# Attention heads of a fused transformer layer: key-major probabilities from a second score matmul, instead of transposing query-major ones

## The chip, the cores and the metric

The kernel runs on one Trainium2 chip as one program on all 8 cores. Each core has one sequence of its own (2048 tokens, model width 4096) and no core talks to another. The time of a run is the device time of the slowest core in microseconds (us). The cores 0 to 3 are on one die of the chip, 4 to 7 on the other.

## The reference, cut to what matters

```python
x = x + 0.5 * ffn(layernorm(x))      # 4096 x 4096 matmul, router, LoRA experts
x = x + attn(layernorm(x))
x = x + 0.5 * ffn(layernorm(x))
# attn, for one head of 32 (S = 2048 tokens):
q = rmsnorm(x @ wq_a.T) @ wq_b.T     # 128 wide: 64 plain + 64 with rope
k, v = rmsnorm(ckv) @ wkv_b.T, ...   # k: 64 plain + 64 shared rope; v: 128
scores = q @ k.T * softmax_scale     # 2048 x 2048, causal
attn   = softmax(scores)
out    = attn @ v
```

The change touches only what follows q, k and v of a head: causal softmax and the product with v.

## The kernel before, in words

The program is written engine by engine, with semaphores set by hand; every engine runs its list strictly in order, so the order in which the code emits instructions is the order of the work. Its stages are: statistics and normalisation, feed-forward, the low-rank projections of the attention, `emit_p35` (normalises the compressed keys, loads the cosine and sine tables), `emit_heads` (32 heads), the output projection, and a second feed-forward. The change touches `emit_heads`, and adds a constant and its load.

One head in `emit_heads` (the lines are those of the kernel before) has two parts.

**Projections** (unchanged by the diff). All of them go through one PSUM bank, `pbC`, with a ScalarE copy behind each: q in four blocks of 8 matmuls (L1067, copy L1171), rope on q in four blocks (a 64x64 matmul L1078, then three VectorE operations L1248, L1251, L1254), k in four blocks (L1085 and L1089, copy L1174), v in four blocks (L1097, copy L1177).

**Attention.** The 16 row blocks i of 128 queries each see i+1 blocks of 128 keys. These are cut into chunks of at most 512 keys (`_chunks`), 40 per head. Four PSUM banks `SLOT` hold scores of a chunk.
- TensorE (function `t`): the scores of each chunk (L1145) with queries on the partitions, plus a 128x128 matmul that adds the causal mask on the diagonal (L1151). Two rows later `emit_tp(i)` transposes the finished probabilities of the row in 128x128 pieces, as matmuls against the identity (L1119, 136 per head), into the banks `pbA` and `pbB` in turn. After every fourth row `emit_pv(J)` multiplies 512 queries with v (L1131, 4J+4 matmuls per J).
- VectorE (function `v`): the negated maximum of each chunk (`reduce_max`, L1292), the maximum over chunks (L1295), then `emit_fin`: four tiny operations for the denominator (L1263 to L1271) and a scaling of the probabilities for each chunk (L1276).
- ScalarE (function `sc`): exp of each chunk with the chunk's own maximum as bias, and the row sum as a by-product (L1223), a tiny exp per row (L1183), and copies of the transposed pieces from `pbA`/`pbB` to SBUF (L1209).

The three engines hand each row to each other, and a row's steps are spread over three iterations of the loop, so that they overlap. Scores may run four chunks ahead of the exp:

```python
if gseq >= 4:
    te.wait_ge(ns.sG.sem, g0 + gseq - 3)     # exp of four chunks ago is done
```

## Time and profile before

| what | us |
|---|---|
| median of 3 runs (lowest, highest) | 9088.95 (9045.17, 9130.27) |
| the profiled execution, its own time | 9045.17 |
| its span on core 5, the slowest | 9043.6 |
| its span on core 2, the fastest | 8670.7 |
| busy in that span: TensorE, VectorE, ScalarE | 5979.0, 2633.8, 1821.5 |

The span runs from the first to the last instruction of a core. Busy time is the time in which an engine has an instruction in work. The granted clock is the share of TensorE's full speed that the chip allowed: 1.00 is 2.4 GHz and 0.50 is 1.2 GHz. The heads stage lasts from 2210.0 to 6065.6 us on core 5.

### The profile page before, as it was taken

To read this page: it belongs to the slowest core of one execution; us is meant where nothing else is said; L and a number is where in the kernel's file an instruction comes from. 1 tells how busy PE (TensorE), PEld (TensorE's weight loads), DVE (VectorE), ACT (ScalarE), POOL (GpSimd) and SP (SyncE) were. 2 spreads that over 40 slices of the span, in tenths; PEclk is the share of its full clock that TensorE was granted. 3 is DMA by queue.
4 is the path that set the end of the run, shared out by engine and by line. 5 is a ranking of instruction groups with operands and counts; after the bars stand their busy time and mean duration, and the time that the engine had idled before them with its cause. 6 is when DMAs were issued, how large, how long until landed. Compare 5 with 4: busy or idle time off the path is not lost.

```text
span 9043.6 us, 88474 instructions; the slowest of 8 cores (8670.7 to 9043.6 us)
## 1 busy us (share of the span) xinstructions
PE 5979.0 (66%) x25428; PEld 2610.5 (29%) x25428; DVE 2633.8 (29%) x7483; ACT 1821.5 (20%) x4918; POOL 221.8 (2%) x422
## 2 busy tenths in 40 slices
PE   3289995375555555555555555547888873399999
PEld 1134442132222222222222222223333331134443
DVE  3410002411444444444444444440000004400000
ACT  0000000001444444444444444440000000000000
POOL 0000000000000000000000000000000000000000
...
DMA packets 205017, 454.16 MB, mean 50 GB/s; under 512 B 27585, under 2 KB 49474, under 8 KB 204162
## 3 DMA queue, kind: packets, MB, share of 16 engines
...
q8 instruction: 218, 3.57, 0.2%
...
## 4 chain that ended last, share of the span: by engine, by line
PE 57%; DVE 17%; issue 9%; ACT 8%; DMA 7%; DVEq 1%; SPq 0%; ACTq 0%; POOL 0%; POOLq 0%
PE scores L581 11%; PE scores L1397 6%; DVE lgf L1292 5%; PE pbD L1131 5%; ACT A L1209 3%; PE pbC L1067 3%; PE pbA L581 3%; PE pbD L581 3%; PE pbC L581 3%; PE pbB L581 3%; DMA Ff<-fw_wo 2%; PE scores L1145 2%; DVE Dn L331 2%; DVE A L335 2%; PE pbA L1397 2%
## 5 line engine op out<-in xcount | busy, mean ns | idle before, releaser
L1292 DVE TENSOR_REDUCE lgf<-scores 128x1 f32<-128x512 f32 (+3 forms) x1280 | 708.5, 603 | 968.9 <-PE scores L1151 543.6
L581 PE MATMUL scores<-A,Ff 128*128 128x512 bf16 x4096 | 985.1, 408 | 0.0
L1223 ACT ACTIVATE A<-scores,lgf 128x512 bf16<-128x512 f32 (+3 forms) x1280 | 784.3, 621 | 825.7 <-DVE lgf L1292 378.1
L1119 PE MATMUL pbA<-ident_bf,A 128*128 128x128 bf16 x2304 | 333.8, 288 | 667.9 <-ACT A L1209 443.4
L1397 PE MATMUL scores<-A,Ff 128*128 128x512 bf16 x2048 | 545.9, 439 | 125.0 <-DMA Ff<-fw_wo 125.0
L1131 PE MATMUL pbD<-A 128*128 128x512 bf16 (+3 forms) x1280 | 450.9, 530 | 232.9 <-ACT A L1209 232.9
L581 PEld LDWEIGHTS scores<-A,Ff 128*128 128x128 bf16 x4096 | 423.1, 103 | 556.6 <-issue 315.0
...
L1145 PE MATMUL scores<-A 128*128 128x512 bf16 (+3 forms) x1280 | 511.4, 505 | 32.3 <-ACT A L1223 25.6
L1119 PE MATMUL pbB<-ident_bf,A 128*128 128x128 bf16 x2048 | 313.9, 289 | 247.6 <-ACT A L1209 158.2
L1119 PEld LDWEIGHTS pbA<-ident_bf,A 128*128 128x128 bf16 x2304 | 210.1, 126 | 797.3 <-issue 793.4
L1276 DVE TENSOR_SCALAR A<-A,lgf 128x512 bf16<-128x512 bf16 (+3 forms) x1280 | 357.1, 329 | 57.0 <-DVE lgf L1271 2.8
L1209 ACT CAST A<-pbA 128x512 bf16<-128x512 f32 (+2 forms) x640 | 348.8, 545 | 76.2 <-PE pbA L1119 72.6
L1397 PEld LDWEIGHTS scores<-A,Ff 128*128 128x128 bf16 x2048 | 222.7, 109 | 448.2 <-issue 394.2
L602 DVE TENSOR_TENSOR Cf<-Cf,scores 128x512 f32<-128x512 f32 x128 | 85.4, 686 | 915.1 <-PE scores L587 509.7
L1209 ACT CAST A<-pbB 128x512 bf16<-128x512 f32 (+3 forms) x640 | 326.5, 510 | 9.9 <-PE pbB L1119 3.1
L1067 PE MATMUL pbC<-Dn,A 128*128 128x512 bf16 x1024 | 261.0, 401 | 90.4 <-ACT A L1171 80.2
L288 PE MATMUL scores<-A,ones_bf 128*1 128x512 bf16 x384 | 171.2, 446 | 210.1 <-DVE Dn L278 210.1
L1131 PEld LDWEIGHTS pbD<-A 128*128 128x128 bf16 x1280 | 161.3, 133 | 514.5 <-issue 504.3
L1119 PEld LDWEIGHTS pbB<-ident_bf,A 128*128 128x128 bf16 x2048 | 196.7, 129 | 319.4 <-issue 301.5
L364 PE MATMUL scores<-stat_m,ones_f 1*128 1x512 f32 x24 | 24.5, 1121 | 387.3 <-ACT stat_r L350 387.3
L1397 PE MATMUL pbA<-A,Ff 128*128 128x512 bf16 x512 | 159.9, 482 | 175.5 <-DMA Ff<-fw_wo 175.5
...
## 6 DMA issues: line engine op xcount, KB each, us to landing
Cf<-x0t SPq DMA_DIRECT2D x128, 256.0 KB, 3.5
...
x1t<-Cf SPq DMA_DIRECT2D x128, 256.0 KB, 5.8
Cf<-x1t SPq DMA_DIRECT2D x128, 256.0 KB, 3.9
...
x2t<-Cf SPq DMA_DIRECT2D x128, 256.0 KB, 3.9
Cf<-x2t SPq DMA_DIRECT2D x128, 256.0 KB, 3.3
```

What stands on the lines that cost most here:

```text
L331: ns.ve_edge(ve, ve.tensor_tensor(ns.Dn[:, D_SPARE:D_SPARE + 512], A[:, off:off + 512], ns.mrbf[:, 0:512], op=AluOpType.subtract))
L335: i = ns.ve_edge(ve, ve.tensor_tensor(A[:, off:off + 512], ns.Dn[:, D_SPARE:D_SPARE + 512], ns.mrbf[:, 512:1024], op=AluOpType.mult))
L581: i = te.matmul(banks[c] if ob % 2 else banks[c][:, 0:512], Ff[:, (si % 2) * 2048 + k * 128:(si % 2) * 2048 + (k + 1) * 128], A[:, dglob * ...
L1067: i = te.matmul(ns.pbC[:, 0:512], A[:, A_WQB + par * 1024 + kk * 128:A_WQB + par * 1024 + (kk + 1) * 128], Dn[:, kk * 2048 + c * 512: kk * ...
L1119: mmi = te.matmul(pb[:, mi * 128:(mi + 1) * 128], A[:, pr(h, i) + tau * 128:pr(h, i) + (tau + 1) * 128], ns.ident_bf[:], start=True, stop= ...
L1131: i = te.matmul(CTX[:, c0:512] if CTX is not ns.pbD else ns.pbD[:, c0:512], A[:, vv(h) + tau * 128:vv(h) + (tau + 1) * 128], A[:, A_PT + t ...
L1145: mmi = te.matmul(SLOT[gseq % 4][:, 0:N], A[:, qf(h) + i * 128:qf(h) + (i + 1) * 128], A[:, kf(h) + kc:kf(h) + kc + N], start=True, stop=n ...
L1209: ns.sEv.inc(se.copy(dst, srcp))
L1223: ns.sG.inc(se.activation(A[:, pr(h, i) + kc:pr(h, i) + kc + N], SLOT[(h * D_G + seq) % 4][:, 0:N], AF.Exp, bias=ns.lgf[:, L_NM + par * 4 ...
L1276: ns.sVe.inc(ve.tensor_scalar(A[:, pr(h, i) + kc:pr(h, i) + kc + N], A[:, pr(h, i) + kc:pr(h, i) + kc + N], ns.lgf[:, L_SC + par * 4 + k:L ...
L1292: ns.sVs.inc(ve.reduce_max(ns.lgf[:, L_NM + par * 4 + k:L_NM + par * 4 + k + 1], SLOT[gsl][:, 0:N], axis=AX, negate=True))
L1397: i = te.matmul(banks[c][:, 0:512] if ob % 2 == 0 else banks[c], Ff[:, (si % 2) * 2048 + kk * 128:(si % 2) * 2048 + (kk + 1) * 128], A[:, ...
```

## The change

The probabilities are no longer transposed. For each head they are computed directly with the keys on the partitions, in a second pass of score matmuls, once the maxima of 512 queries are known.

- The first pass remains for its maxima alone: chunk scores, mask and `reduce_max`. It has two PSUM slots (`QS`) and waits for the maximum of two chunks ago. The maximum over chunks goes to a bf16 column of `mrbf`, and a small matmul (`nmtp`) turns it into 128 numbers of a row in `pbB` or `pbD`; after four rows ScalarE copies the row of 512 to SBUF (`nrow`).
- After the rows 5, 9, 13 and 15 comes a second pass, `_drain(J)`, over the 4J+4 key blocks tau of the query group J. Per tau: a score matmul over 512 queries (`T`), for the four diagonal tau a 512-wide mask matmul (from the new constant `triT`), a matmul of one row of ones with `nrow` that subtracts the maxima, exp without bias or sum into one of six buffers, a matmul with a column of ones that sums the denominator (`den`) and the product with v (`pv`), both two tau behind and always over all 512 queries.
- The denominator of the group goes through Ln and Exp(-x) on ScalarE (one row of 512), is spread over the partitions by an fp32 matmul with ones (`dbrd`), copied to `Cf` by VectorE and multiplied into the result as it leaves PSUM (`jev`).
- Gone are the transposes and their copies, `emit_fin` and `emit_alpha`.
- One more load in `emit_p35`: `triT`, 128 x 1024.

The core of the diff, with what repeats left out:

```diff
@@ emit_heads: the order
+    def _drain(J):
+        last = 4 * J + 3
+        for t in range(last + 1):
+            SCHED.append(("T", J, t))
+            if t >= 2:
+                SCHED.append(("den", J, t - 2))
+                SCHED.append(("pv", J, t - 2))
+        for t in (last - 1, last):
+            SCHED.append(("den", J, t))
+            SCHED.append(("pv", J, t))
+    for _i in range(NT):
+        for _k in range(len(_chunks(_i))):
+            SCHED.append(("q", _i, _k))
+        if _i >= 2:
+            SCHED.append(("nmtp", _i - 2))
+            if (_i - 2) % 4 == 3:
+                _drain((_i - 2) // 4)
+        if _i in (8, 12):
+            SCHED.append(("dbrd", (_i - 8) // 4))
+    SCHED += [("nmtp", 14), ("nmtp", 15), ("dbrd", 2)]
+    _drain(3)
+    SCHED.append(("dbrd", 3))
@@ emit_heads: TensorE
-            for i in range(NT):
-                chs = _chunks(i)
-                for k, (kc, N) in enumerate(chs):
...
-                    if gseq >= 4:
-                        te.wait_ge(ns.sG.sem, g0 + gseq - 3)
...
-                j = i - 2
-                if j >= 0:
-                    emit_tp(j)
-                    if j % 4 == 3:
-                        emit_pv(j // 4)
+                if kind == "q":
...
+                    if GQ >= 2:
+                        i2, k2 = CL[(GQ - 2) % 40]
+                        te.wait_ge(ns.sVs.sem,
+                                   B((GQ - 2) // 40, vs0, D_VS) + vs_idx[("mx", i2, k2)])
...
+                elif kind == "T":
...
+                    if tau == 0:
+                        te.wait_ge(ns.sEv.sem, hb_ev + ev_nr(J))
+                    if GT >= 2:
+                        te.wait_ge(ns.sG.sem, g0 + GT - 1)
+                    sl = TSL[GT % 2]
+                    te.matmul(sl[:, 0:512], A[:, kf(h) + tau * 128:kf(h) + (tau + 1) * 128],
+                              A[:, qf(h) + J * 512:qf(h) + (J + 1) * 512],
+                              start=True, stop=False)
+                    r = tau - 4 * J
+                    if r >= 0:
+                        te.matmul(sl[:, 0:512], ns.ident_bf[:],
+                                  triT[:, (3 - r) * 128:(3 - r) * 128 + 512],
+                                  start=False, stop=False)
+                    ns.sMM.inc(te.matmul(sl[:, 0:512], ns.onesr_bf[:], nrow(gj),
+                                         start=False, stop=True))
+                elif kind == "den":
...
+                    te.wait_ge(ns.sG.sem, g0 + GT + 1)
+                    i2 = te.matmul(MB[gj % 2][64:65, 0:512], ns.ones_bf[:], pts(GT),
+                                   start=(tau == 0), stop=(tau == 4 * J + 3))
...
+                elif kind == "pv":
...
+                    ns.sMM.inc(te.matmul(CTX[:, 0:512],
+                                         A[:, vv(h) + tau * 128:vv(h) + (tau + 1) * 128],
+                                         pts(GT), start=(tau == 0), stop=(tau == 4 * J + 3)))
+                elif kind == "dbrd":
...
+                    te.wait_ge(ns.sSc.sem, hb_sc + 2 * J + 2)
+                    ns.sMM2.inc(te.matmul(MB[gj % 2][:, 0:512], ns.ones_f32[:], rrow(gj)[:],
+                                          start=True, stop=True))
@@ emit_heads: ScalarE
+                ns.sEv.inc(se.copy(nrow(gj), MB[gj % 2][0:1, 0:512]))
...
+                    ns.sG.inc(se.activation(pts(GT), TSL[GT % 2][:, 0:512], AF.Exp))
...
+                ns.sSc.inc(se.activation(lrow[:], MB[gj % 2][64:65, 0:512], AF.Ln))
+                se.wait_ge(ns.sSc.sem, hb_sc + 2 * J + 1)
+                ns.sSc.inc(se.activation(rrow(gj)[:], lrow[:], AF.Exp, scale=-1.0))
@@ emit_heads: VectorE
+                if i in (9, 13):
+                    jev((i - 9) // 4)
+            jev(2)
+            jev(3)
```

How the order moves on TensorE, at the group J=1 of a head. In the kernel before, after the chunk scores (L1145, L1151) of row 9 come the transposes of row 7 (L1119, sources in A, the identity moving) and then the product with v (L1131):

```order
L1145 MATMUL scores<-A 128x512 x2
L1145 MATMUL scores<-A 128x256
L1151 MATMUL scores<-tri_sb,ident_bf 128x128
L1119 MATMUL pbA<-ident_bf,A 128x128 x4
L1119 MATMUL pbB<-ident_bf,A 128x128 x4
L1131 MATMUL pbD<-A 128x512 x5
L1131 MATMUL pbD<-A 128x384
L1131 MATMUL pbD<-A 128x256
L1131 MATMUL pbD<-A 128x128
```

In the changed kernel, from the same place (L1158 and L1162 are the chunk scores, L1174 is `nmtp`), the second pass begins: L1186 is the score matmul of `T`, L1194 its row of ones with `nrow` (in Ff), L1201 `den` and L1213 `pv`; for a diagonal tau L1191, the mask, stands between L1186 and L1194:

```order
L1158 MATMUL scores<-A 128x512 x2
L1158 MATMUL scores<-A 128x256
L1162 MATMUL scores<-tri_sb,ident_bf 128x128
L1174 MATMUL pbD<-ident_bf,mrbf 1x128
L1186 MATMUL scores<-A 128x512
L1194 MATMUL scores<-Ff,onesr_bf 128x512
L1186 MATMUL scores<-A 128x512
L1194 MATMUL scores<-Ff,onesr_bf 128x512
L1186 MATMUL scores<-A 128x512
L1194 MATMUL scores<-Ff,onesr_bf 128x512
L1201 MATMUL pbD<-A,ones_bf 1x512
L1213 MATMUL pbA<-A 128x512
```

Eight transposes and eight products with v (four of them narrow) become 8 tau of four full-width matmuls, and a fifth on the four diagonal ones; no chunk scores of later rows stand among them.

On ScalarE, in the rows 3 to 5 of a head before, exp (L1223), the tiny exp of the row (L1183) and the copies of the transposes (L1209) alternate:

```order
L1223 ACTIVATE A,lgf<-scores,lgf 128x512 [waits sVs,sMM2,sVe]
L1183 ACTIVATE lgf<-lgf 128x1 [waits sVs]
L1209 CAST A<-pbB 128x2x128 [waits sMM,sMM2]
L1223 ACTIVATE A,lgf<-scores,lgf 128x512 [waits sVs,sMM2,sVe]
L1223 ACTIVATE A,lgf<-scores,lgf 128x128 [waits sVs,sMM2,sVe]
L1183 ACTIVATE lgf<-lgf 128x2 [waits sVs]
L1209 CAST A<-pbA 128x3x128 [waits sMM,sMM2]
```

Now a group is one row copy (L1243), its exps (L1251), and Ln and Exp of the denominator (L1257, L1259):

```order
L1243 CAST Ff<-pbB 1x512 [waits sMM2,sMM]
L1251 ACTIVATE A<-scores 128x512 [waits sMM] x12
L1257 ACTIVATE rowB<-pbB 1x512 [waits sMM2]
L1259 ACTIVATE rowA<-rowB 1x512 [waits sSc]
L1243 CAST Ff<-pbD 1x512 [waits sMM2,sMM]
L1251 ACTIVATE A<-scores 128x512 [waits sMM] x16
```

ScalarE has nothing to do between the groups, and VectorE's maxima are all that stands beside the first pass.

## Rows read from the trace of the kernel before

**Rows 1.** Spans and granted clock of the cores.
```profile
core 5: 9043.6 us, clock 0.717
...
die 0 (median of its cores): 8677.6 us, clock 0.758
```

**Rows 2.** PE, PEld, DVE, ACT, POOL busy, PEclk, DMA: projections, attention, heads stage.
```profile
4388.40:4426.20 37.80, 20.06 (x84) 7.78 (x83) 6.79 (x13) 6.45 (x11) 0.00 (x0) 0.67 0.01 4
4426.20:4508.30 82.10, 44.93 (x234) 23.40 (x233) 48.19 (x163) 47.35 (x137) 1.59 (x3) 0.58 0.05 10
2210.00:6065.60 3855.60, 2101.35 (x9984) 1002.26 (x9984) 1758.49 (x5632) 1720.73 (x4737) 47.77 (x90) 0.61 0.04 8
```

**Rows 3.** Costliest group of VectorE: busy, mean ns | idle before, releaser.
```profile
L1292 DVE TENSOR_REDUCE lgf<-scores 128x1 f32<-128x512 f32 (+3 forms) x1280 | 708.5, 603 | 968.9 <-PE scores L1151 543.6
```

**Rows 4.** Timeline, PE and DVE handing over PSUM in rope; start us, us.
```profile
4401.35 0.42 DVE L1254 TENSOR_TENSOR A<-Ff 64x512 bf16<-64x512 bf16 x1
...
4401.92 0.60 PE L1078 MATMUL pbC<-A,p_hi 64*64 64x512 bf16 x1 [2.12 <-DVE A L1254]
4402.77 0.42 DVE L1248 TENSOR_TENSOR Ff<-A 64x512 bf16<-64x512 bf16 x1 [0.99 <-PE pbC L1078]
```

**Rows 5.** Groups by shape, 4400 to 4900 us: the 512-wide maximum.
```profile
L1292 DVE TENSOR_REDUCE lgf<-scores 128x1 f32<-128x512 f32 x112 | 71.5, 683 | 53.1 <-PE scores L1145 52.6 <-issue 0.3
```

**Rows 6.** Timeline, TensorE and ScalarE handing over PSUM, k projection.
```profile
4411.16 0.63 PE L1089 MATMUL pbC<-A,ident_bf 64*64 64x512 bf16 x1
4411.89 0.59 ACT L1174 CAST A<-pbC 128x512 bf16<-128x512 f32 x1 [12.71 <-PE pbC L1089]
...
4412.62 0.61 PE L1085 MATMUL pbC<-A 128*64 128x512 bf16 x1 [0.82 <-ACT A L1174]
```

**Rows 7.** Timeline, PE alone: product with v (J=2), and a transpose after a pause.
```profile
4480.54 4.01 PE L1131 MATMUL pbD<-A 128*128 128x512 bf16 x12 [1.03 <-ACT A L1209]
...
4489.37 0.42 PE L1119 MATMUL pbA<-ident_bf,A 128*128 128x128 bf16 x4 [3.24 <-ACT A L1209]
```

**Rows 8.** Around the same place: PE busy (x), PEclk, DMA share, GB/s.
```profile
4482.00:4483.00 1.00, 1.00 (x3) 0.50 0.00 0
...
4484.00:4485.00 1.00, 1.00 (x7) 0.81 0.00 0
4489.00:4490.00 1.00, 0.57 (x6) 0.81 0.00 0
...
4491.00:4492.00 1.00, 1.00 (x7) 0.50 0.38 131
```

**Rows 9.** Timeline, PE: q projection of the first head, and of a later one.
```profile
2218.88 3.57 PE L1067 MATMUL pbC<-Dn,A 128*128 128x512 bf16 x8 [0.82 <-ACT A L1171]
2223.28 3.57 PE L1067 MATMUL pbC<-Dn,A 128*128 128x512 bf16 x8 [0.82 <-ACT A L1171]
...
4391.19 1.89 PE L1067 MATMUL pbC<-Dn,A 128*128 128x512 bf16 x8 [0.82 <-ACT A L1171]
```

**Rows 10.** Timeline, PE: 128 matmuls in both feed-forwards; core 0's windows in the second.
```profile
529.17 27.79 PE L581 MATMUL scores<-A,Ff 128*128 128x512 bf16 x128
...
8025.06 33.78 PE L581 MATMUL scores<-A,Ff 128*128 128x512 bf16 x128
...
8000.00:8600.00 600.00, 600.00 (x2781) 272.01 (x2780) 55.91 (x84) 0.00 (x0) 0.00 (x0) 1.00 0.38 111
```

**Rows 11.** Timeline: one-row Ln, Exp and fp32 matmul in emit_p35.
```profile
2168.11 0.63 ACT L905 ACTIVATE rowB<-rowA 1x512 f32<-1x512 f32 x1
...
2169.61 2.04 PE L892 MATMUL pbA<-stat_r,ones_f 1*128 1x512 f32 x2 [4.17 <-ACT stat_r L906]
```

**Rows 12.** Timeline, PE: an 8-row stationary tile, then a 128-row one.
```profile
371.24 0.58 PE L496 MATMUL pbB<-Dn,r_bf 8*128 8x512 bf16 x1 [0.81 <-ACT Dn L422]
371.75 0.61 PE L499 MATMUL pbC<-A,Ef 128*128 128x512 bf16 x1
```

**Rows 13.** DMA issues of emit_p35: KB each, us to landing.
```profile
A<-sin_t POOLq DMA_DIRECT2D x2, 256.0 KB, 8.9
```

More of the change, by code:

```diff
@@ L34 @@
 A_PT = 22528
+A_TRI_T = 25600
 A_WQB = 30720
@@ L856, in gcs @@
         ns.sO.inc(gp.dma_start(out=A[64:128, A_SIN2:A_SIN2 + 2048], in_=ns.dr["sin_t"]), 16)
+        ns.sO.inc(gp.dma_start(out=A[:, A_TRI_T:A_TRI_T + 1024], in_=ns.dr["triT"]), 16)
     sq0, sqf0, st0 = ns.sSq.n, ns.sSqf.n, ns.sStat.n
@@ new lines, in emit_heads @@
+    TAUS = [(J, t) for J in range(4) for t in range(4 * J + 4)]
+    TIDX = {jt: s for s, jt in enumerate(TAUS)}
+    CL = [(i, k) for i in range(NT) for k in range(len(_chunks(i)))]
+    CIDX = {ik: s for s, ik in enumerate(CL)}
+    SCHED = []
+    def _drain(J):
[8 more added lines that the diff above has]
+            SCHED.append(("pv", J, t))
@@ new lines, in emit_heads @@
+    for _i in range(NT):
[10 more added lines that the diff above has]
+    SCHED.append(("dbrd", 3))
+    mm_i, mm2_i = {}, {}
+    n1, n2 = 12, 4
+    for ev in SCHED:
+        if ev[0] in ("q", "T", "pv"):
+            n1 += 1
+            mm_i[ev] = n1
+        elif ev[0] == "nmtp":
+            n2 += 1
+            mm2_i[ev] = n2
+        elif ev[0] == "den":
+            if ev[2] == 4 * ev[1] + 3:
+                n2 += 1
+                mm2_i[("denl", ev[1])] = n2
+        elif ev[0] == "dbrd":
+            n2 += 1
+            mm2_i[ev] = n2
@@ L1011, in emit_heads @@
+    assert n1 == D_MM and n2 == D_MM2, (n1, n2)
     vs_idx = {}
     n = 0
-    for i in range(NT):
-        for k in range(len(_chunks(i))):
+    for _i in range(NT):
+        for _k in range(len(_chunks(_i))):
             n += 1
-            vs_idx[("mx", i, k)] = n
+            vs_idx[("mx", _i, _k)] = n
         n += 1
-        vs_idx[("ms", i)] = n
+        vs_idx[("ms", _i)] = n
     assert n == D_VS
-    ve_nrm = lambda i, k: 4 + _CS[i] + k + 1
     ev_q = lambda c: c + 1
@@ L1032, in vv, with pts, nrow, rrow @@
     def vv(h): return A_V if h % 2 == 0 else A_V2
[L1033 to L1036 removed]
+    QS = [ns.scores[:, 0:512], ns.scores[:, 512:1024]]
+    TSL = [ns.scores[:, 1024:1536], ns.scores[:, 1536:2048]]
+    CTX = ns.pbA
+    MB = [ns.pbB, ns.pbD]
     KPS = ns.pbC
[L1038 removed]
+    triT = A[:, A_TRI_T:A_TRI_T + 1024]
+    def pts(GT): return A[:, A_PT + (GT % 6) * 512:A_PT + (GT % 6 + 1) * 512]
+    def nrow(gj): return Ff[0:1, 1024 + 512 * (gj % 2):1536 + 512 * (gj % 2)]
+    def rrow(gj): return ns.rowA if gj % 2 == 0 else ns.rowB
+    def cfd(gj): return Cf[:, 512 * (gj % 2):512 * (gj % 2) + 512]
     def g(gp):
@@ L1124, in emit_pv @@
-            def emit_pv(J):
-                te.wait_ge(ns.sEv.sem, hb_ev + ev_g(_cg(4 * J + 3) - 1))
-                te.wait_ge(ns.sEv.sem, hb_ev + 12)
-                if h > 0 or J > 0:
-                    te.wait_ge(ns.sRES.sem, hb_res + J)
-                for tau in range(4 * J + 4):
-                    c0 = max(0, tau - 4 * J) * 128
-                    i = te.matmul(CTX[:, c0:512] if CTX is not ns.pbD else ns.pbD[:, c0:512],
-                                  A[:, vv(h) + tau * 128:vv(h) + (tau + 1) * 128],
-                                  A[:, A_PT + tau * 512 + c0:A_PT + (tau + 1) * 512],
-                                  start=(tau == 0), stop=(tau == 4 * J + 3))
-                ns.sMM.inc(i)
@@ L1231, in sc @@
-            emit_evacs(NT - 2)
-            emit_evacs(NT - 1)
+            for J in range(4):
+                gj = 4 * h + J
+                se.wait_ge(ns.sMM2.sem, hb_mm2 + mm2_i[("nmtp", 4 * J + 3)])
+                if gj >= 2:
+                    ph2, J2 = divmod(gj - 2, 4)
+                    se.wait_ge(ns.sMM.sem, B(ph2, mm0, D_MM) + mm_i[("T", J2, 4 * J2 + 3)])
+                ns.sEv.inc(se.copy(nrow(gj), MB[gj % 2][0:1, 0:512]))
+                for tau in range(4 * J + 4):
+                    GT = h * 40 + TIDX[(J, tau)]
+                    se.wait_ge(ns.sMM.sem, hb_mm + mm_i[("T", J, tau)])
+                    if GT >= 6:
+                        ph3 = (GT - 6) // 40
+                        J3, t3 = TAUS[(GT - 6) % 40]
+                        se.wait_ge(ns.sMM.sem, B(ph3, mm0, D_MM) + mm_i[("pv", J3, t3)])
+                    ns.sG.inc(se.activation(pts(GT), TSL[GT % 2][:, 0:512], AF.Exp))
+                lrow = rrow(gj + 1)
+                se.wait_ge(ns.sMM2.sem, hb_mm2 + mm2_i[("denl", J)])
+                if gj >= 1:
+                    phx, Jx = divmod(gj - 1, 4)
+                    se.wait_ge(ns.sMM2.sem, B(phx, mm20, D_MM2) + mm2_i[("dbrd", Jx)])
+                ns.sSc.inc(se.activation(lrow[:], MB[gj % 2][64:65, 0:512], AF.Ln))
+                se.wait_ge(ns.sSc.sem, hb_sc + 2 * J + 1)
+                ns.sSc.inc(se.activation(rrow(gj)[:], lrow[:], AF.Exp, scale=-1.0))
@@ L1636, in host_prep @@
     out["ones_row"] = np.ones((1, 128), dtype=np.float32)
+    triT = np.zeros((128, 1024), dtype=np.float32)
+    kkg, cg = np.meshgrid(np.arange(128), np.arange(1024), indexing="ij")
+    triT[kkg > cg - 384] = NEG_BIG
+    out["triT"] = triT
     R2 = np.zeros((8, 128), dtype=np.float32)
```

223 lines of the change are left out of this document (67 added, 156 removed).

## The prediction

> **What bounds the kernel now.** I read first the spans of the cores, then the busy time by stage, then the costliest groups, and last the timeline of one head. The spans [rows 1] show the slowest core at 9043.6 us with a clock of 0.717, where the other die has 8677.6 and 0.758. The execution itself took 9045.2 us, 1.6 more than the span, and lies 43.8 us under the median of the runs (9088.95); sums are made against 9045.2 and 43.8 is added at the end.
>
> The windows [rows 2] give the heads stage 3855.6 us, 120.5 per head, 43% of the span. One head has two parts: from its first q matmul (4388.4) to its first chunk scores (4426.2) 37.8 us of projections, and 82.1 us of attention. In the attention no engine is full: TensorE 44.9 us, VectorE 48.2, ScalarE 47.4. Of the idle time before VectorE's maxima, 968.9 us over the span, more than half ends on TensorE's scores [rows 3], and a transpose after 3.2 us of pause waits for ScalarE's copy [rows 7]. So the attention is bound by hand-overs round three engines, and a change can win by shortening that ring, or lose by putting more work on one engine of it. Note TensorE's clock of 0.58 in the attention: it works mostly at 1.2 GHz.
>
> **What goes.** 136 transposes, 40 ScalarE copies, 40 exps with sum and four small VectorE steps per row. In TensorE columns: the first pass has 28 chunks of 512 and 12 narrower ones, with masks 19,456 columns; transposes 136 x 128 = 17,408; product with v 17,408. That is 54,300 columns per head. The changed kernel keeps 19,456, and adds per tau `T`, ones, `den` and `pv` (4 x 512, 40 tau), 16 wide masks, 2,048 for `nmtp` and four fp32 spreads: 176 x 512 = 90,100 in the second pass alone. The waits for the ring go, but TensorE's load rises by more than 60,000 columns per head, 25 us at 2.4 GHz and 50 at 1.2. TensorE is now what the second pass is bound by; ScalarE needs 0.59 us per exp (the 128x512 copy of [rows 6]) where TensorE needs at least 4 x 0.216 = 0.86 per tau, and VectorE is idle there. So these two cost nothing in the second pass.
>
> **The change, part by part, per head.**
>
> *Projections:* untouched, 37.8. Their q part runs at full clock if dense matmuls stand before them, as the product with v does now and the last second pass will. If not, each block of 8 takes 3.57 plus a wait of 0.82 [rows 9], 4.39, where a later head has 1.89 and the wait, 2.71: 4 x 1.68 = 6.7 more. Bounds 37 to 45.
>
> *First pass:* with four slots TensorE ran ahead; with two, chunk n waits for the maximum of n-2. From the end of a VectorE operation to the start of the next that needs a fresh 512-column matmul is 4401.77 to 4402.77, 1.00 us at 1.2 GHz [rows 4], and a maximum takes 0.683 [rows 5]. Two chunks in turn: (1.00 + 0.68) / 2 = 0.84 per full chunk. Scaled by width, and with 0.11 for each mask, 40 chunks come to 31.6. The pass is cut in four by the second passes; at three cuts two maxima fall under the second pass (about -1.5 each), but each restart costs the filling of the slots (+1). At 2.4 GHz a chunk is 0.11 cheaper. I take 29, bounds 26 to 33. The small operation that joins a row's maxima lies in the slack of the slots.
>
> *Second pass:* its four groups have 20, 36, 52 and 68 matmuls of 512, 176 in all. At full clock 128 matmuls take 27.63 (27.79 less the overlapping tail [rows 10]), 0.216 each; on this die in the second feed-forward 33.6, 0.263. At 1.2 GHz one is 0.427. So the whole is 38.0, 46.2 or 75.1 us. Which clock? In [rows 7, 8] the product with v of J=2 begins at 4480.5 after a pause and stays at 0.50 for 3 us of unbroken matmuls, then gets 0.81; after the pause before 4489.4 (3.2 us) it is still 0.81, and from 4491 it is 0.50, though TensorE is now busy. The new first pass leaves TensorE idle for about half of each 0.84 us, so I expect that the clock falls in each, and that each second pass starts at 1.2 GHz. I take 4 us at 1.2 GHz for each of the four: 16 us, about 34 matmuls. The other 142 run between 0.216 and 0.263; the middle, leaning to full clock, is 0.235: 33.4. Then the stationary tile changes its height twice per tau, 128 rows to one and back. After an 8-row tile the next matmul started 0.51 later instead of 0.427 [rows 12], so up to 0.1 per change at 1.2 GHz and less at full clock; I take 0.1 per tau, 3.8. Sum 53.2; bounds 38 (full clock from the start, changes free) and 75.1 + 15 = 90.
>
> *Starts of the groups:* `T` waits for `nrow`: a small matmul, a ScalarE copy and the way back. From the start of such a matmul to the start of the next behind the copy is 4411.16 to 4412.62 [rows 6], 1.46 for 512 columns, 1.1 for 128. Three times in full, and once behind `dbrd`(2): 3.4. Bounds 2 to 6.
>
> *End of the head:* `dbrd`(3) waits for Ln and Exp of a row. From the start of such a Ln to the matmul behind the Exp is 1.50 [rows 11]; the last `pv` covers 0.2: 1.3. Queued behind it is the next head's q projection, and so everything.
>
> *Four fp32 spreads:* 2.04 each at 1.2 GHz [rows 11], about half at full clock. Two stand among chunk scores, where half a chunk's time is slack (1 each), one before the last group (2), one at the end (1): 5. Bounds 2.5 to 8. `jev`'s copy and product (0.7 each) run under a second pass; without that cover they would cost 4 x 1.5 = 6.
>
> *Table and constants:* Ln and Exp follow each other without a table load [rows 11]; I count none. `triT` lands with the tables, where sin_t takes 8.9 us [rows 13]: 0 to 9 once, 3 taken.
>
> Sum: 37.8 + 29 + 53.2 + 3.4 + 1.3 + 5 = 129.7 against 120.5, 9.2 more. Times 32 is 294, plus 3: 9045.2 + 297 = 9342, and with 43.8 the forecast is 9386 us, 3.3% slower. A measurement tells about 1% (91 us) from no change.
>
> The sum of the low bounds is 37 + 26 + 38 + 2 + 1.3 + 2.5 = 106.8, the high one 45 + 33 + 90 + 6 + 1.3 + 8 = 183; both need every term at one end.
>
> On a stream of weight loads and matmuls, the Trainium skill ("TensorE: Matmul & The Clock Gate", Back-to-back issue gap) states about 131 ns per 512-column matmul. By that the second pass would be 23 us at full clock and the change a clear gain; the trace's 128 matmuls in 27.6 us are such a stream and show 216 ns, so I give it no chance.
>
> **The rivals.**
>
> *A. The clock stays up (not slower).* If the first passes, between 4 and 10 us long, do not let the clock fall, the second passes are 38 + 4 = 42, the first 27, the spreads 3.5, and the head 37.8 + 27 + 42 + 3.4 + 1.3 + 3.5 = 115.0: 32 x -5.5 = -176, so 9045 - 173 + 44 = 8916. For it: a later head's q projection pauses 0.82 in every 2.71 us and keeps the full clock [rows 9]. Against it: the first pass pauses more than half of its time at full clock (0.22 of 0.73 us), and [rows 8] show a fall after a pause. It decides from the second group on: about half of the 16 us must run at full clock for the result to be the time of before.
>
> *B. The second pass never leaves 1.2 GHz.* The first head's q projection [rows 9] is busy 3.57 of every 4.39 us and stays at 0.50 for both blocks. If the tile changes and one-row tiles leave such holes, the second pass is 75.1 + 8 = 83, the first pass 31, spreads 7, projections 44.5: 44.5 + 31 + 83 + 3.4 + 1.3 + 7 = 170.2, 49.7 x 32 = 1590, so 10,682. Against it: there is no wait in the second pass, and 0.2 of 1.9 us is a smaller hole.
>
> *C. The slower die is held at 13/16.* If the denser second passes bring the 0.263 of [rows 10] everywhere, 142 matmuls take 37.3 instead of 33.4, and the q projection 1.5 more: 5.4 x 32 = 173, so 9559. The trace shows both: core 5 at 0.81 in [rows 8] and in the second feed-forward, core 0 at 1.00 there with TensorE busy all of 600 us [rows 10]. The same page of the Trainium skill (Seeing it yourself) says that three cores of a die with dense matmuls bring 13/16; by it the time would be C's, and core 0's row speaks against it as a rule for every die.
>
> *D. Nothing to measure.* Terms between A and the forecast: the second pass at 47 and the first at 28 give 122.5, 9152.
>
> **Chances.** Forecast 0.45, C 0.17, B 0.12, A 0.14, D 0.12. The likeliest case alone spans 9200 to 9560. The range for 8 in 10 leaves out most of A, and B: 9000 to 9950. Faster by over 1% (under 8998): A, 0.14. Within 1%: D, 0.12. Slower: 0.74.
>
> **What would show it.** In the profile after: heads stage about 4150 us on core 5; 176 matmuls per head in the second pass, first at 0.427, then at 0.216 to 0.263 apart; granted clock 0.5 at the start of each `T` stream and higher 4 us in; between chunk maxima 0.84 us; TensorE waiting for VectorE in the first pass and for nothing in the second; ScalarE's and VectorE's busy time well below 47 us per head. Wrong would be: gaps in the second pass that end on ScalarE's exp, a table load per group, or chunk scores that follow each other faster than 0.7 us.

## The result, and the profile after

The changed kernel takes 10193.94 us (median of 12 runs, 9983.89 to 10351.07), where the kernel before, run beside it, takes 9041.71 (14 runs, 8864.36 to 9153.05). The ratio of these medians is 1.127. In many executions of every kernel here one die, or both, shows a lower granted clock and ends later, as in [rows 1], so the verdict is taken from the executions without that, and beside the times I give the median span of the cores of a die without it ("free die" below). The ratio is then 1.109, 95% interval 1.102 to 1.116: 11% slower. The prediction said slower, 9386 us, with a range of 9000 to 9950.

For the kernel before, the free die takes 8670 to 8702 us in nearly every run (8684 taken), for the changed one 9948 to 9998 (9976 taken). The difference is 1292 us, 40.4 per head.

The spans of the cores in the profiled execution of the changed kernel (10013.97 us) answer to [rows 1]; the two dies agree:

```profile
core: us from the first to the last instruction, mean granted TensorE clock
core 5: 10012.2 us, clock 0.737
...
die 0 (median of its cores): 9982.6 us, clock 0.738
die 1 (median of its cores): 9998.2 us, clock 0.738
```

The windows of the heads stage, then of one head's parts in order, answer to [rows 2]. The columns are the stretch, its length, busy time (and instructions) of PE, PEld, DVE, ACT and POOL, the granted clock, the DMA share and GB/s:

```profile
2209.00:7350.30 5141.30, 4138.20 (x10752) 976.35 (x10752) 1169.33 (x2430) 1220.13 (x2049) 47.75 (x90) 0.62 0.03 6
```

```profile
4455.40:4493.00 37.60, 19.86 (x81) 7.58 (x81) 7.48 (x14) 6.45 (x11) 0.00 (x0) 0.67 0.01 4
4493.00:4499.60 6.60, 4.62 (x22) 1.64 (x20) 4.61 (x14) 1.16 (x2) 1.59 (x3) 0.50 0.42 56
4499.60:4509.60 10.00, 10.00 (x21) 1.74 (x22) 0.00 (x0) 2.62 (x5) 0.00 (x0) 0.50 0.01 2
4509.60:4519.90 10.30, 7.92 (x21) 1.93 (x20) 6.60 (x15) 1.56 (x3) 0.00 (x0) 0.50 0.00 0
4519.90:4538.00 18.10, 18.09 (x37) 3.36 (x38) 1.05 (x2) 5.01 (x9) 0.00 (x0) 0.50 0.02 7
4538.00:4551.30 13.30, 10.29 (x25) 2.21 (x23) 8.94 (x19) 1.56 (x3) 0.00 (x0) 0.50 0.00 1
4551.30:4574.60 23.30, 23.21 (x53) 4.46 (x54) 1.23 (x2) 7.19 (x13) 0.00 (x0) 0.59 0.02 6
4574.60:4583.10 8.50, 5.37 (x17) 1.46 (x15) 5.34 (x10) 1.76 (x3) 0.00 (x0) 0.87 0.00 1
4583.10:4613.50 30.40, 30.40 (x69) 5.58 (x68) 1.38 (x2) 9.62 (x17) 0.00 (x0) 0.59 0.01 5
4613.50:4615.90 2.40, 1.12 (x3) 0.29 (x2) 0.00 (x0) 1.15 (x2) 0.00 (x0) 1.00 0.00 0
```

The heads stage takes 5141 us (3856 before), 160.7 per head; the prediction had looked for about 4150. The head shown takes 160.5. Projections: 37.6. The four parts of the first pass with the starts and spreads in them: 6.6 + 10.3 + 13.3 + 8.5 = 38.7. The four groups of the second pass, where TensorE is busy all the time: 10.0 + 18.1 + 23.3 + 30.4 = 81.8. The end: 2.4. The mean of all heads differs a little from this one: over 8 cores and 32 heads the second pass takes 79.8 and the projections 40.3. In the first two groups the clock is 0.50 (1.2 GHz) throughout, in the others 0.59: busy from end to end, TensorE still stays at its lower level.

The costliest groups of the page answer to [rows 3]. Columns: line, engine, operation, out<-in, count | busy, mean ns | idle before, releaser:

```profile
L1301 DVE TENSOR_REDUCE lgf<-scores 128x1 f32<-128x512 f32 (+3 forms) x1280 | 735.5, 607 | 2220.8 <-PE scores L1158 1669.7
L1251 ACT ACTIVATE A<-scores 128x512 bf16<-128x512 f32 x1280 | 764.1, 597 | 1651.0 <-PE scores L1194 1651.0
L1186 PE MATMUL scores<-A 128*128 128x512 bf16 x1280 | 757.0, 591 | 94.6 <-ACT Ff L1243 93.2
L1194 PE MATMUL scores<-Ff,onesr_bf 1*128 1x512 bf16 x1280 | 719.1, 562 | 0.0
```

Here the maxima's idle time has grown from 968.9 to 2220.8 us, nearly all of it waiting for TensorE; the exps wait 1651.0 us for the row of ones. TensorE waits for nothing at L1194, and at L1186 for the row of maxima (93.2 in all, 0.97 at a time). So TensorE now bounds the second pass, as forecast, and neither ScalarE nor VectorE is near.

Last, the timeline of TensorE inside the group J=1 (start, duration as the profile models it, engine, line). The distance of starts is what to read:

```profile
4523.11 0.59 PE L1201 MATMUL pbD<-A,ones_bf 128*1 128x512 bf16 x1
4523.63 0.61 PE L1213 MATMUL pbA<-A 128*128 128x512 bf16 x1
4524.03 0.63 PE L1186 MATMUL scores<-A 128*128 128x512 bf16 x1
4524.60 0.60 PE L1194 MATMUL scores<-Ff,onesr_bf 1*128 1x512 bf16 x1
4525.13 0.59 PE L1201 MATMUL pbD<-A,ones_bf 128*1 128x512 bf16 x1
```

One tau takes 2.02 us where four matmuls of 0.427 are 1.71. `pv` to `T`, both with 128x128 tiles, is 0.40; the three steps whose tile changes shape are 0.57, 0.53 and 0.52. A change costs 0.1 each, and there are three per tau, for `den`'s tile has one column and counts as another shape too.

### The profile page after: what moved, and what is told of

The parts are those of the page before. It is cut to its first block, busy times and chain, and to the rows that moved or that the text cites. A ratio compares the mean times of both kernels' runs of the same rounds, so it can differ in the third digit from the quotient of the medians.

```text
span 10012.2 us, 79131 instructions; the slowest of 8 cores (9970.5 to 10012.2 us)
## 1 busy us (share of the span) xinstructions
PE 7678.8 (77%) x26196; PEld 2506.3 (25%) x26196; DVE 2047.4 (20%) x4284; ACT 1320.9 (13%) x2230; POOL 222.3 (2%) x423
## 3 DMA queue, kind: packets, MB, share of 16 engines
q14 instruction: 156, 1.28, 0.0%
## 4 chain that ended last, share of the span: by engine, by line
PE 71%; DVE 13%; DMA 6%; issue 5%; ACT 4%; DVEq 1%; SPq 0%; ACTq 0%; POOL 0%; POOLq 0%
PE scores L584 9%; PE scores L1194 6%; PE pbA L1213 6%; PE scores L1186 6%; DVE lgf L1301 5%; PE scores L1397 5%; PE pbD L1201 3%; PE pbC L1109 3%; PE pbB L1201 2%; PE pbA L584 2%; DMA Ff<-fw_wo 2%; PE pbD L584 2%; PE pbC L584 2%; PE pbB L584 2%; PE scores L1191 2%
## 5 line engine op out<-in xcount | busy, mean ns | idle before, releaser
L1301 DVE TENSOR_REDUCE lgf<-scores 128x1 f32<-128x512 f32 (+3 forms) x1280 | 735.5, 607 | 2220.8 <-PE scores L1158 1669.7
L1251 ACT ACTIVATE A<-scores 128x512 bf16<-128x512 f32 x1280 | 764.1, 597 | 1651.0 <-PE scores L1194 1651.0
L584 PE MATMUL scores<-A,Ff 128*128 128x512 bf16 x4096 | 889.3, 379 | 0.0
L1186 PE MATMUL scores<-A 128*128 128x512 bf16 x1280 | 757.0, 591 | 94.6 <-ACT Ff L1243 93.2
L1158 PE MATMUL scores<-A 128*128 128x512 bf16 (+3 forms) x1280 | 526.6, 444 | 260.9 <-DVE lgf L1301 252.7
L1194 PE MATMUL scores<-Ff,onesr_bf 1*128 1x512 bf16 x1280 | 719.1, 562 | 0.0
L1213 PE MATMUL pbA<-A 128*128 128x512 bf16 x1280 | 688.9, 538 | 0.0
L1397 PE MATMUL scores<-A,Ff 128*128 128x512 bf16 x2048 | 474.8, 397 | 118.6 <-DMA Ff<-fw_wo 118.6
L1201 PE MATMUL pbD<-A,ones_bf 128*1 128x512 bf16 x768 | 392.7, 511 | 0.0
L1194 PEld LDWEIGHTS scores<-Ff,onesr_bf 1*128 1x128 bf16 x1280 | 123.7, 97 | 882.6 <-issue 882.6
L1158 PEld LDWEIGHTS scores<-A 128*128 128x128 bf16 x1280 | 128.5, 105 | 656.7 <-issue 635.2
L1191 PE MATMUL scores<-A,ident_bf 128*128 128x512 bf16 x512 | 278.2, 543 | 0.0
L1201 PE MATMUL pbB<-A,ones_bf 128*1 128x512 bf16 x512 | 272.8, 533 | 0.0
```

Source lines behind the costliest of these rows:

```text
L584: i = te.matmul(banks[c] if ob % 2 else banks[c][:, 0:512], Ff[:, (si % 2) * 2048 + k * 128:(si % 2) * 2048 + (k + 1) * 128], A[:, dglob * ...
L1158: mmi = te.matmul(sl[:, 0:N], A[:, qf(h) + i * 128:qf(h) + (i + 1) * 128], A[:, kf(h) + kc:kf(h) + kc + N], start=True, stop=not diag)
L1186: te.matmul(sl[:, 0:512], A[:, kf(h) + tau * 128:kf(h) + (tau + 1) * 128], A[:, qf(h) + J * 512:qf(h) + (J + 1) * 512], start=True, stop=F ...
L1191: te.matmul(sl[:, 0:512], ns.ident_bf[:], triT[:, (3 - r) * 128:(3 - r) * 128 + 512], start=False, stop=False)
L1194: ns.sMM.inc(te.matmul(sl[:, 0:512], ns.onesr_bf[:], nrow(gj), start=False, stop=True))
L1201: i2 = te.matmul(MB[gj % 2][64:65, 0:512], ns.ones_bf[:], pts(GT), start=(tau == 0), stop=(tau == 4 * J + 3))
```

## The experiments

The question is what holds the clock at 1.2 GHz in a stretch that is busy throughout. In the changed kernel it rises late or never. From the profile of each run, over all 8 cores and 32 heads (256 groups of each J), come three things: the mean length of each group, from its first score matmul to the end of its last `pv`; the time from its start until the granted clock leaves 0.50; and the time per head that the four groups together spend at 0.50. Three theories:

- **R**: matmuls with a tile of few rows (the one row of ones) do not raise the clock as full ones do.
- **C**: the same for a tile of few columns (the one column of `den`).
- **H**: the holes of 0.1 us at the changes of shape keep it down.

What the runs gave, in one table (durations in us; "tau" is one non-diagonal tau at 1.2 GHz, "group lengths" are for J=0 to 3, "rise" is the median time from the group's start for J=1, 2, 3, "at 0.50" is per head):

| kernel | changes of shape per tau | tau | group lengths | rise | at 0.50 | span, free die |
|---|---|---|---|---|---|---|
| before | - | - | - | - | - | 8684 |
| changed | 3 | 2.02 | 10.2, 15.4, 23.6, 30.6 | 11.3, 19.6, 25.1 | 66.8 | 9976 |
| e1: 128 rows | 2 | 1.86 | 7.8, 12.1, 16.6, 21.3 | 4.5, 4.2, 3.8 | 18.5 | 9122 |
| e2: `den` 128 columns | 2 | 1.93 | 9.3, 14.3, 20.9, 26.9 | 11.2, 14.7, 22.3 | 54.9 | 9684 |
| e3: both | 0 | 1.71 | 6.8, 10.5, 14.5, 17.8 | 4.4, 5.4, 3.6 | 18.3 | 8970 |
| e4: pairs of tau | 1.5 | 1.87 | 9.9, 14.3, 20.9, 27.2 | 8.2, 16.0, 22.6 | 57.0 | 9665 |
| e7: 64 rows | 3 | 2.02 | 9.6, 14.7, 19.3, 25.3 | 11.1, 10.6, 13.0 | 41.3 | 9558 |
| e9: 32 rows | 3 | 2.02 | 9.8, 14.7, 22.1, 26.1 | 10.5, 15.3, 8.8 | 50.3 | 9690 |
| e11: 128 rows, more holes | 4 | 2.07 | 8.2, 12.9, 18.5, 23.6 | 4.0, 6.0, 6.0 | 20.5 | 9448 |
| e8: no row of ones | 2 | 1.48 | 6.9, 10.8, 14.4, 18.0 | 6.0, 6.6, 7.5 | 25.0 | 8992 |

The rise varies from head to head: in the changed kernel the middle half of the J=2 groups lies between 17.5 and 22.6 us, and a single group is no measure. In e3's profile the groups take 50.5 us per head on the longer die (9373) and 48.8 on the other (8964), so a difference of 2 us between rows means little. The 9122 of e1 comes from one die of one execution.

**e1: the row of ones as a full tile.** `nrow`'s partition 0 stays as it is and the other 127 hold zeros; the tile has ones in row 0 and zeros below. The sum is the same, the tile is 128x128.

```diff
-                    ns.sMM.inc(te.matmul(sl[:, 0:512], ns.onesr_bf[:], nrow(gj),
+                    ns.sMM.inc(te.matmul(sl[:, 0:512], SEL, nfull(gj),
...
+        ns.ve_edge(ve, ve.memset(Ff[:, 1024:2048], 0.0))
+        ns.ve_edge(ve, ve.memset(SEL, 0.0))
+        ns.ve_edge(ve, ve.memset(SEL[0:1, :], 1.0))
```

> Edit: the row of ones with the maxima runs as a matmul of 128 rows (stationary tile with ones in row 0 and zeros below, moving tile with zeros below the maxima) instead of one row. Same number of matmuls. In the changed kernel a tau of the second pass takes 2.02 us at 1.2 GHz, 0.31 of it at three changes of the tile's shape (128x128, 1x128, 128x1, 128x128), and the clock rises only in the diagonal part. Theory H (the pauses at the shape changes keep the clock down): one or two changes go, 1.81 to 1.92 us per tau, pauses of 5 to 11%, and the clock rises some 4 us into each group; second pass 80 us per head down to about 57, whole run down by about 700 us (9300). Theory R (matmuls of one row do not count as work for the clock): the same rise. Theory C (matmuls of one column do not count): no rise, only the changes' 0.1 to 0.2 us per tau, down by 130 to 260 us (9750 to 9900).

Measured: 9494.83 and 9525.32 us, free die 9122 (9300 had been expected, of R and of H alike, so this run speaks only against C). It brings 854 us, two thirds of all that was lost: one change of shape less is 0.16 per tau, at most 6.4 us per head or 205 us, and the rest goes with the clock, which has risen within 6.2 us in every group that began at 0.50.

**e2: `den` with 128 columns**, so that the thin column goes and the thin row stays.

```diff
-                    i2 = te.matmul(MB[gj % 2][64:65, 0:512], ns.ones_bf[:], pts(GT),
+                    i2 = te.matmul(MB[gj % 2][:, 0:512], ONES, pts(GT),
```

> Edit: den is a matmul with a 128-column tile of ones (the sums land on all 128 partitions) instead of one column; the row of ones stays one row. Theory H: the change between den and pv goes, 1.92 us per tau, pauses of 11%; the clock rises in most groups, down by 400 to 700 us. Theory R: no rise, one change fewer, down by about 130 us (9870). Theory C: the clock rises, down by about 700 us.

Measured: 9702.74 and 10058.49, free die 9684. One change of shape less per tau gives 0.09 x 40 = 3.6 us per head at 1.2 GHz; the whole is 9.1 per head (292 us, where R had 130 and H and C at least 400). The clock still rises late, at 14.7 us in J=2, but earlier than the 19.6 of the changed kernel. So C falls as the main cause; whether the hole or the column brings the small rest, this run does not tell.

**e3: both tiles full.**

> Edit: both, so that every matmul of the second pass has a 128x128 tile. All theories: no pauses, 1.71 us per tau at 1.2 GHz, and if pauses or thin tiles were the cause the clock rises within about 4 us of each group's start: second pass 80 us per head down to about 51, run down by 900 us (9100), about the time of before. If the clock stays down for another reason: only 0.31 us per tau, 12 us per head, down by 400 us (9600).

Measured: 9005.56 to 9619.74 (four runs), free die 8970. Against e1 it saves 152 us, 4.8 per head: 40 tau with two changes less, 0.12 per tau. Full tiles throughout, and the kernel is still 286 us slower than before.

**e4: tau in pairs**, the thin tiles kept: two score matmuls, two rows of ones, two `den`, two `pv`. Three changes per two tau. In the diff `S` is the score matmul and `T` is left with the row of ones.

```diff
+        for t in range(0, last + 3, 2):
+            if t < last:
+                SCHED.extend([("S", J, t), ("S", J, t + 1), ("T", J, t), ("T", J, t + 1)])
+            if t >= 2:
+                SCHED.extend([("den", J, t - 2), ("den", J, t - 1), ("pv", J, t - 2), ("pv", J, t - 1)])
```

> Edit: all tiles keep their shapes, but two tau go together (two score matmuls, two rows of ones, two den, two pv), so that there are three shape changes per two tau. Theory H: 1.86 us per tau, pauses of 8%, the clock rises some 4 us into each group, down by 500 to 700 us. Theories R and C: the share of thin matmuls is unchanged, so no rise; only 0.15 us per tau, 6 us per head, down by about 200 us (9800). This tells H from R and C.

Measured: 9694.21 and 10010.69, free die 9665. Its tau is 1.87 long, as e1's is, so its holes add up to as much; but it is 543 us slower than e1, and its clock mostly rises at 16 to 20 us in J=2 where e1's rises at 4. Here is the start of such a group, busy as e1's is; columns: stretch and length, PE busy (and matmuls), granted clock, DMA share and GB/s:

```profile
2787.90:2791.90 4.00, 4.00 (x10) 0.50 0.00 0
...
2795.90:2799.90 4.00, 4.00 (x10) 0.50 0.00 0
2799.90:2803.90 4.00, 4.00 (x17) 0.96 0.00 0
```

The sum of the holes cannot be what differs between the two. Against the changed kernel e4 saves 9.7 us per head, of which 40 x 0.15 = 6.0 are the holes' own length: with the one-row tile in place, fewer holes help the clock a little, and no more.

**e7 and e9: 64 and 32 rows**, a dose between 1 and 128. The number of changes stays at three. Against e1 the edit of e7 is:

```diff
-                    ns.sMM.inc(te.matmul(sl[:, 0:512], SEL, nfull(gj),
+                    ns.sMM.inc(te.matmul(sl[:, 0:512], SEL[0:64, :], nfull(gj)[0:64, :],
```

> Edit: the row of ones with the maxima as a matmul of 64 rows (ones in row 0, zeros below). The tile still changes its shape three times per tau as in the changed kernel (about 2.02 us per tau at 1.2 GHz), so pauses and number of matmuls are the same; only the rows in use differ. Theory H (pauses): no early rise of the clock, time as the changed kernel, 10000 in an undisturbed run. Theory R (a matmul of one row counts little): the clock rises some 5 us into each group, second pass about 62 instead of 82 us per head, 9400 to 9550.

> Edit: the same with 32 rows. Theory H: as the changed kernel, 10000. Theory R: if what counts is the rows in use, between one row (10000) and 64 rows; if the one-row matmul already counts as a whole strip of 32 rows, no different from one row, 10000. Guess: later rises than with 64 rows, 9700.

Measured: 64 rows 9578.45 to 9853.47, free die 9558; 32 rows 9709.66 and 10004.69, free die 9690. With tau unchanged at 2.02, 64 rows bring 418 us of e1's 854, 32 rows 286. With 1, 32, 64 and 128 rows the clock rises in J=2 at 19.6, 15.3, 10.6 and 4.2 us, the groups spend 66.8, 50.3, 41.3 and 18.5 us per head at 0.50, and of the 256 groups J=0 the clock never rises in 252, 91, 17 and none. (With 32 rows J=3 is uneven, a quarter of its groups above 24.8 us and half below 8.8.)

**e11: 128 rows, and more holes than the changed kernel has.** A matmul with one moving column and `den`'s thin tile stands between `T` and the ones, so that there are four changes per tau.

```diff
+                    te.matmul(MB[gj % 2][96:97, 0:1], ns.ones_bf[:],
+                              A[:, kf(h) + tau * 128:kf(h) + tau * 128 + 1],
+                              start=True, stop=True)
+                    ns.sMM.inc(te.matmul(sl[:, 0:512], SEL, nfull(gj),
```

> Edit on top of e1 (ones as 128 rows): a matmul of one column against a one-column tile stands between the score matmul and the row of ones, which does no work but forces two more changes of the tile's shape: four per tau, more pause than the changed kernel has (three), with every moving tile on 128 rows. Theory H (pauses keep the clock down): as in the changed kernel the clock rises only in the diagonal part; with 2.1 to 2.2 us per tau at 1.2 GHz 10100 to 10300. Theory R (rows in use): the clock rises 4 to 6 us into each group as in e1 (9524), and only the pauses' own time is added, some 0.2 us per tau, 8 us per head: 9750 to 9800.

Measured: 9470.73 and 9782.5, free die 9448. H had 10100 to 10300; R had 9750 to 9800, reckoned from e1's longer execution, and the longer one here is 9782.5. This is the run that decides. The windows below follow a J=2 group from its start in four kernels, until its clock has risen; the columns are those of e4's. The changed kernel:

```profile
core 5: us, PE busy (x), PEclk, DMA share, GB/s
4551.30:4555.30 4.00, 3.91 (x8) 0.50 0.10 33
4555.30:4559.30 4.00, 4.00 (x9) 0.50 0.02 4
4559.30:4563.30 4.00, 4.00 (x9) 0.50 0.00 0
4563.30:4567.30 4.00, 4.00 (x9) 0.50 0.00 0
4567.30:4571.30 4.00, 4.00 (x10) 0.59 0.00 0
4571.30:4575.30 4.00, 3.87 (x14) 1.00 0.00 0
```

64 rows (e7; this group rises at 8.4 us, its median is 10.6):

```profile
3041.40:3045.40 4.00, 3.94 (x8) 0.50 0.10 33
3045.40:3049.40 4.00, 4.00 (x9) 0.50 0.02 4
3049.40:3053.40 4.00, 4.00 (x14) 0.94 0.00 0
3053.40:3057.40 4.00, 4.00 (x16) 1.00 0.00 0
```

128 rows (e1):

```profile
2959.60:2963.60 4.00, 3.80 (x9) 0.50 0.11 37
2963.60:2967.60 4.00, 4.00 (x16) 0.97 0.00 0
```

128 rows and four changes (e11):

```profile
2884.00:2888.00 4.00, 3.84 (x11) 0.50 0.10 33
2888.00:2892.00 4.00, 4.00 (x15) 0.73 0.00 0
2892.00:2896.00 4.00, 4.00 (x18) 1.00 0.01 2
```

And the timeline of e11 shows that the holes are there: from `T` to `T` it is 2.07 us, and between `T` and the ones stands the small matmul, 0.52 behind `T` and 0.10 ahead of the ones:

```profile
2742.87 0.59 PE L1188 MATMUL scores<-A 128*128 128x512 bf16 x1
2743.39 0.17 PE L1196 MATMUL pbB<-A,ones_bf 128*1 128x1 bf16 x1
2743.49 0.61 PE L1199 MATMUL scores<-Ff,A 128*128 128x512 bf16 x1
2744.03 0.58 PE L1206 MATMUL pbB<-A,ones_bf 128*1 128x512 bf16 x1
2744.54 0.61 PE L1218 MATMUL pbA<-A 128*128 128x512 bf16 x1
2744.94 0.63 PE L1188 MATMUL scores<-A 128*128 128x512 bf16 x1
```

A tau is longer than in the changed kernel (2.07 against 2.02 at 1.2 GHz) and has more holes, and yet the clock has risen within 8.2 us in every group of all heads, and the kernel is 528 us faster than the changed one. Under H it had to be slower. Against e1 the extra holes cost 326 us, 10.2 per head, of which 40 x 0.21 = 8.4 are their own length: holes cost their length and little more. R stands: it is the rows that the tile uses. The short tile was one matmul in four or five here; other mixes were not run. The rows added in e1, e7, e9 and e11 hold nothing but zeros, so it isn't what is multiplied either.

**e8: no row of ones.** The maxima are not subtracted, so a whole matmul per tau is left out.

> Edit on top of the changed kernel: the matmul of the row of ones is left out, so the exp is taken without subtracting the maxima (the quotient is the same as long as no exp overflows); the first pass and the row copy still run. Three matmuls and two shape changes per tau, den still one column. Theory R: all matmuls have 128 rows, the clock rises 4 to 6 us into each group; second pass 82 to about 46 us per head, 8850 to 8950. Theory H: pauses are 0.15 of 1.43 us, 10%, as in e1: the same. Without a rise it would be 1.43 us per tau, 64 us, 9450.

Measured: 9005.29 to 9272.19 (four runs), free die 8992. Tau is 1.48, and the clock rises at 4 to 8 us with `den`'s thin tile as one matmul of three: again not C. A miss in size: only 130 us under e1, 4.1 per head, though 40 matmuls of at least 0.216 (8.6 us) are gone. The clock rises up to 4 us later than in e1 (medians for J=1 to 3), which gives part of it back. Why later no run here settles; e11, with more holes, rises at 4 to 6 us, so the thin column is the likelier of the two.

**e5: no spread.** On top of e3: `den` with a 128x128 tile of ones already puts the sum on all partitions, so Ln and Exp work on 128 partitions into `Cf`, and `dbrd`, its wait at the head's end and VectorE's copy go.

```diff
-        if _i in (8, 12):
-            SCHED.append(("dbrd", (_i - 8) // 4))
...
-                ns.sSc.inc(se.activation(lrow[:], MB[gj % 2][64:65, 0:512], AF.Ln))
+                ns.sSc.inc(se.activation(cfd(gj), MB[gj % 2][:, 0:512], AF.Ln))
```

> Edit on top of e3 (all tiles 128x128): den lands on all 128 partitions, so Ln and Exp run on 128 partitions straight into Cf, and the fp32 spread, its VectorE copy and the wait at the head's end go. Ledger of the changed kernel: spreads 2.0 three times and 1.0, wait at the end 1.3 per head, 8.4 less what is slack. Expected 6 to 8 us per head less than e3 (9005 in its fastest run): 8760 to 8810, just faster than before (8835 to 9054).

Measured: 9124.22 to 9194.54 (four runs), free die 8680: 290 us under e3, 9.1 per head. I had priced the spreads at 5 and the end at 1.3. The profiles of the two give 4 us for the spreads among the first passes, 2.3 at the end, and 2.1 in the projections, which now begin at the higher clock. A free die is thereby as fast as before, but each of the four executions is longer than all three of the kernel before beside it (8707.24 to 8928.47), and the verdict over them is slower, a ratio of 1.053 (95% interval 1.042 to 1.063).

**e6 and e12: the diagonal narrowed.** On top of e5, every matmul and exp of a diagonal tau works on the columns at and right of the diagonal block, and its mask is 128 wide. e12 is the same kernel once more.

```diff
+                    c0 = max(0, r) * 128
-                    te.matmul(sl[:, 0:512], A[:, kf(h) + tau * 128:kf(h) + (tau + 1) * 128],
-                              A[:, qf(h) + J * 512:qf(h) + (J + 1) * 512],
+                    te.matmul(sl[:, c0:512], A[:, kf(h) + tau * 128:kf(h) + (tau + 1) * 128],
+                              A[:, qf(h) + J * 512 + c0:qf(h) + (J + 1) * 512],
```

> Edit on top of e5: in the four diagonal tau of a group the score matmul, the maxima row, exp, den and pv run only over the queries from the diagonal on (512, 384, 256, 128), the mask over 128 columns. 18,400 columns fewer per head, most of them at 2.4 GHz late in a group: 8 to 12 us per head, 8400 to 8550, 5% faster than before. If exp (ScalarE) becomes the bound in the narrow tau: 5 us per head less, 8620.

> The kernel of e6 again (nothing left out of the computation), for an interval: 8480 to 8500 in an undisturbed run, 2 to 4% faster than before.

Measured: e6 8486.61 and 8936.87, where the kernel before had 8707.24, 8718.75 and 8928.47; e12 8667.91 to 8921.11 (six runs), before 8701.16 to 9286.6 (seven). A free die takes 8467 to 8482 us, 2.4% under the 8684 of before; the median of the six e12 runs (8833.52) is 1.7% under its own kernel before (8986.69), without an interval. So this version beats the kernel before by 2.4% where a die is free, and how much it gains over many executions stays open.

**e10: no first pass.** On top of e6: no maxima, nothing subtracted, three score slots and two banks for the result. It leaves out the subtraction of the maxima and so shows what the change could have brought if no maximum were needed.

> Edit on top of e6: the first pass, the maxima, nmtp, the row copy and the maxima row are left out (exp without subtracting the maxima, which bounds nothing if scores grow large), three score slots and two context banks. Per head: projections 37.7, second pass 54,300 columns, 25 us at 2.4 GHz and 4 to 5 us more for the start at 1.2 GHz, shape changes none, one start: about 68 to 72 us against 160 in the changed kernel and 120 before: 7050 to 7250, 19% faster than before. If exp (40 of 0.2 to 0.6 us, some 22 us) and its hand-over bound the second pass, 5 us more: 7400.

Measured: 7089.91 to 7463.07 (four runs), free die 7069, 18.6% under before. Two lines of its page, the busy times and the clock in 40 slices (the heads stand in the 13th to 25th):

```profile
PE 4977.0 (70%) x21939; PEld 2177.3 (31%) x22356; DVE 1163.2 (16%) x2368; ACT 1126.2 (16%) x2102; POOL 222.9 (3%) x423
...
PEclk8579999975977787787878878799999885799999
```

Its clock in the heads is mostly 7 or 8 tenths, where the changed kernel's is 5 or 6. e6 needs 112.8 us per head, this 68.7. Of the 44 between them, the first pass with its starts is 33; the other 11 are the second pass, 41.9 against 30.8, which has lost its row of ones and runs in one piece. No repair of the second pass touches the 33.

## Why the prediction was right or wrong

- **Projections, 37.8:** 40.3 in the mean, within the bounds. In the head shown, and in 103 of the 256, they take 37.5 to 38.1 with a q part at the higher clock, as said; but 130 take over 41. On core 5 the q part of the former has a granted clock of 0.86 to 0.95 and that of the latter 0.63 to 0.71; what decides which it is, no run here shows. One of the long ones, to compare with the window of the projections above:

```profile
4131.75:4174.61 42.86, 24.76 (x81) 8.62 (x81) 7.48 (x14) 6.45 (x11) 0.00 (x0) 0.58 0.01 3
```

- **First pass, starts and three spreads, 29 + 3.4 + 4 = 36.4:** 38.7 in the head shown, 37.6 in the mean. From `nmtp` to `T` it is 1.24 (1.1 taken), 0.97 of it wait. In three of the four parts the clock is 0.50. The bounds hold.
- **End, 1.3, and the last spread, 1:** 1.28 of wait and 1.02 from the spread's start to the next head's in this head. Right:

```profile
4614.89 1.09 PE L1220 MATMUL pbD<-rowB,ones_f 1*128 1x512 f32 x2 [1.28 <-ACT rowB L1259]
4615.91 1.25 PE L1109 MATMUL pbC<-Dn,A 128*128 128x512 bf16 x5
```

- **ScalarE and VectorE hidden, no table load per group:** right. TensorE waits for an exp 0.8 us in the whole kernel, and the only table load at a line of the heads is one in the first head.
- **Second pass, 53.2:** 81.8 in the head shown, 79.8 in the mean. This is the step that failed. Like for like, on a free die, the forecast was 8684 + 297 = 8981, and 9976 was measured: 995 us, of which 26.6 x 32 = 851 are this term. (The forecast of 9386 looks nearer because its base, the slower die of [rows 1], was longer by 360.)
  - "I take 4 us at 1.2 GHz for each of the four" is the wrong term. The forecast had 16 us per head at 1.2 GHz; the groups spend 66.8 there. The 4 us were read from [rows 7, 8], where the product with v, 128x128 tiles alone, left 0.50 after 3 us. The second pass is not that stream: every fourth matmul has a tile of one row. With the one row filled up (e1, e3) the clock does rise 4 to 6 us in, 18 us per head are spent at 0.50, and the groups are 58 and 50 us; so the reading of [rows 8] was right for the stream it came from, and carried to another.
  - "I take 0.1 per tau" for the changes of shape: three changes and 0.31 per tau at 1.2 GHz, as the timeline above shows. I had not counted `den`'s one-column tile as a change of shape, and the 0.08 of [rows 12] for each of two changes was cut to 0.1 per tau for the full clock, where a change costs 0.10 as well (below). That is up to 8 of the 26.6 us; e3 against e1 gives 4.8 for two changes.
- **Rival B** came nearest: 170.2 per head against 160.5, at a chance of 0.12, with 83 for the second pass and no rise of the clock at all. It named "tile changes and one-row tiles" and then argued by the size of the holes ("0.2 of 1.9 us is a smaller hole"). The holes were indeed small, and e11 shows that they do not matter for the clock; what I took as a detail of the holes, the one row, is the cause. The argument against B used the wrong quantity. So the nearest number is in part luck: B had the right outcome by the wrong mechanism.
- **Rival A** (the clock stays up): it does not. After the J=2 group the following 8.5 us of first pass still show 0.87, but the last group begins at 0.50 (as 226 of the 256 do), and stays there for some 24 us without a wait:

```profile
4574.60:4583.10 8.50, 5.37 (x17) 0.87 0.00 1
4583.10:4587.10 4.00, 4.00 (x9) 0.50 0.10 33
...
4603.10:4607.10 4.00, 4.00 (x10) 0.50 0.00 0
4607.10:4611.10 4.00, 4.00 (x14) 0.87 0.01 4
```

- **Rival C** (held at 13/16) is not what happened: in the profiled execution the clock reads 1.00 once it has risen (4571.30 to 4575.30 above).
- **The range** ended at 9950, under the term's own bound of 90 us for the second pass. It had been cut there by giving B little.
- **Slips in the sums**, none of which matters: by width alone the 40 chunks come to 30.3 us and not 31.6 (29 was taken); 16 us at 1.2 GHz hold 37 matmuls and not 34, and 0.1 per tau is 4.0 and not 3.8, together less than 1 us per head; D's 122.5 give 9156 and not 9152.

The Trainium skill ("TensorE: Matmul & The Clock Gate", What's actually happening) puts the clock down to how busy TensorE has been lately. With full tiles the traces agree (e1, e3); with the one-row tile they do not: busy 4.00 of 4.00 us in three windows on end above, and the granted clock is 0.50. The measurement decides: for such tiles the busy time does not tell what clock will be granted.
